# Seven PSUM banks of an attention loop as two slots for maxima and three single-head banks

## What is computed

```python
tokens = x.reshape(B, C, N).transpose(0, 2, 1)
qkv = (tokens @ w_proj + b_proj).reshape(B, N, NUM_HEADS, 3 * HEAD_DIM)
q, k, v = jnp.split(qkv, 3, axis=-1)
attn = jnp.einsum('bihd,bjhd->bijh', q, k) * SCALE
attn = jax.nn.softmax(attn, axis=2)
res = jnp.einsum('bijh,bjhd->bihd', attn, v).reshape(B, N, NUM_HEADS * HEAD_DIM)
out = res @ w_out + b_out + tokens
```

## Time and profile before

| | us |
|---|---|
| median of 3 runs | 3099.82 (3094.11 to 3104.37) |
| the profiled execution | 3101.73 |
| its span | 3100.0 |
| TensorE busy | 2708.6 |
| VectorE busy | 2196.4 |
| ScalarE busy | 1220.1 |
| GpSimd busy | 603.8 |
| mean granted TensorE clock | 0.935 of full |

### The profile page before, as it was taken

The page is one execution under the profiler, slowest core; times in us unless marked ns, Lnnn a source line. Parts: engine busy times, 40 slices in busy tenths (PEclk is TensorE's granted clock), DMA queues, the critical chain, the costliest instruction groups (busy, mean ns, idle before and its releaser), DMA issues.

```text
span 3100.0 us, 42243 instructions
## 1 busy us (share of the span) xinstructions
PE 2708.6 (87%) x14966; PEld 1854.5 (60%) x14966; DVE 2196.4 (71%) x2490; ACT 1220.1 (39%) x1348; POOL 603.8 (19%) x381
## 2 busy tenths in 40 slices
PE   5989979899898898988889888898888899888993
PEld 4447754577545775467754677447764477644772
DVE  4876678766687676867678576785678766787666
ACT  2443325433254333543335333353334533245334
POOL 0520116002160022500224002330024200242011
PEclk8999989999799998999989999899999999899996
DMA  6100050000500005000040001400022000310016
GB/s 154 27 25 1 1 130 1 25 1 14 117 1 25 1 14 117 1 25 1 21 110 1 25 1 38 93 7 19 1 69 62 25 1 1 94 37 25 1 55 244
DMA packets 46388, 124.57 MB, mean 40 GB/s; under 512 B 9792, under 2 KB 21312, under 8 KB 42560
## 3 DMA queue, kind: packets, MB, share of 16 engines
q1 hardware_dynamic: 46144, 121.41, 14.4%
HBM read 43.01 MB, written 23.86 MB: 22 GB/s over the span
## 4 chain that ended last, share of the span: by engine, by line
PE 69%; DVE 10%; ACT 8%; issue 6%; SPq 4%; DMA 3%; DVEq 0%; ACTq 0%
PE tile L1270 23%; PE pv L1270 10%; PE pv L1374 7%; PE tile L1364 6%; PE tile L1342 5%; ACT p L666 4%; PE tile L1515 4%; SPq L452 3%; PE tile L1394 3%; DMA stack<-qk_r 2%; DVE small L877 2%; PE tile L1537 2%; PE tile L1645 2%; PE tile L1564 1%; PE tile L1416 1%
## 5 line engine op out<-in xcount | busy, mean ns | idle before, releaser
L877 DVE TENSOR_REDUCE small<-tile 128x1 f32<-128x1024 f32 x512 | 612.6, 1220 | 125.0 <-PE tile L1342 121.1
L666 ACT ACTIVATE p<-tile 128x1024 f32<-128x1024 f32 x512 | 506.7, 1026 | 457.9 <-PE tile L1364 393.4
L1342 PE MATMUL tile<-stack 96*128 96x512 f32 x1024 | 356.9, 441 | 63.6 <-DMA stack<-qk_r 30.3
L1364 PE MATMUL tile<-stack 112*128 112x512 f32 x1024 | 369.0, 452 | 20.8 <-DVE small L877 14.1
L1270 PE MATMUL tile<-qk_r 128*128 128x512 f32 x1536 | 377.9, 395 | 0.0
L578 POOL TENSOR_TENSOR row_sum<-act 128x256 f32<-128x256 f32 x32 | 42.1, 1335 | 1640.0 <-DVE act L1105 1640.0
L553 POOL TENSOR_TENSOR acc<-acc,p 128x1024 f32<-128x1024 f32 x144 | 344.8, 2416 | 31.2 <-DVE acc L909 29.3
L1270 PEld LDWEIGHTS tile<-qk_r 128*128 128x128 f32 x1536 | 287.1, 188 | 66.4 <-issue 7.7
L1110 DVE TENSOR_TENSOR pl<-p,ph 128x1024 fp32r<-128x1024 f32 x128 | 158.2, 1236 | 238.0 <-ACT p L751 238.0
L1364 PEld LDWEIGHTS tile<-stack 112*128 112x128 f32 x1024 | 175.2, 196 | 241.7 <-issue 85.0
L1342 PEld LDWEIGHTS tile<-stack 96*128 96x128 f32 x1024 | 185.9, 202 | 187.2 <-ACT p L666 110.8
(11 more groups left out here) (277 smaller groups left out, 4256.0 us busy)
## 6 DMA issues: line engine op xcount, KB each, us to landing
stack<-qk_r SPq DMA_DIRECT2D x192, 256.0 KB, 5.0
x_in<-in_x_dram SPq DMA_DIRECT2D x9, 1024.0 KB, 7.6
act<-in_x_dram SPq DMA_DIRECT2D x8, 1024.0 KB, 8.0
x_scratch<-act SPq DMA_DIRECT2D x7, 1024.0 KB, 4.0
z_scratch<-zbuf SPq DMA_DIRECT2D x7, 1024.0 KB, 5.1
stack<-ones SPq DMA_DIRECT2D x8, 512.0 KB, 7.6
w3f<-w3f_scratch SPq DMA_DIRECT2D x8, 512.0 KB, 3.2
fin_rest<-z_scratch SPq DMA_DIRECT2D x3, 1024.0 KB, 12.7
```

Of the source, the lines that this page charges most:

```text
L666: sc.activation(p0[:, jt % DEPTH, pair, :], tile_wait(b, "st0", *u, jt, pair), ACT.Exp, scale=float(D) ** -0.5).then_inc(scalar_done, scal ...
L877: ve.tensor_reduce(maxima[:, h * NT + it:h * NT + it + 1], t[:], X, ALU.max).then_inc(vector_done, vector.one("max0", g, h, it))
L1342: ins = mm(o[:, s], stack[0:IMAX, 0, g, h, it * P:(it + 1) * P], stack[0:IMAX, 1, g, h, s], start=True, stop=True)
L1364: ins = mm(o[:, halves[k]], stack[0:K0, 1, g, h, jt * P:(jt + 1) * P], stack[0:K0, 0, g, h, halves[half]], start=True, stop=True)
```

## The change

- The loop's scores of the first three units are tiles of one head, 128x512, one bank. They rotate over three banks: the two of `tile[2]` and the half of `pv` that the unit doesn't write. `exp0` follows, four a key tile. The last unit keeps pairs.
- Maxima tiles `s0`, and with them the loop's `m0`, `den0` and `ex0`, alternate between `tile[0]` and `tile[1]`. Everything outside the loop, with the last unit, rotates over three tiles as before.
- The order in a key tile is score, score, maximum, maximum, score, score, values.
- `max_rows` on VectorE keeps heads 0 and 1; ScalarE writes heads 2 and 3 in four `max_cols` of 16x256, each with a column of `mask8` as its scale. The maxima's tile is free when both are through.
- `pv0_out` and `max_cols` precede the unit's exponentials on ScalarE.
- `res_lo` moves from VectorE to GpSimd, behind its adds of tile 1, except for the last unit's. Its wait for `res_hi` moves with it.
- The bias of the values is left out of `res_hi` and `res_lo`; its product with the output weights is made once in the setup (4 matmuls, one add, `bvo0`) and added in `x1`.

```diff
+def score_tiles(g, half):
+
+    return 2 if (g, half) == UNITS[-1] else G
...
+def key_tile(g, half):
+
+    if next_unit(g, half):
+        return ("st0", 0), ("st0", 1), ("s0", 0), ("s0", 1), ("st0", 2), ("st0", 3)
+    return ("st0", 0), ("st0", 1)
...
     for u in UNITS:
+        s += [("pv0_out", *last_unit(*u))] if last_unit(*u) else []
+        s += [("max_cols", *u, t) for t in range(HT)]
         for jt in range(NT):
-            s += [("pv0_out", *last_unit(*u))] if last_unit(*u) and jt == 0 else []
-            s += [("exp0", *u, jt, pair) for pair in range(2)]
+            s += [("exp0", *u, jt, k) for k in range(score_tiles(*u))]
             s += [("res_hi", *last_unit(*u))] if last_unit(*u) and jt == 2 else []
...
-            s += [("res_lo", *last)] if last and jt == 3 else []
         if following:
             s += [(n, *following) for n in ("neg_hi", "neg_copy", "neg_lo")]
-            s += [("max_rows", *following, h) for h in range(G)]
+            s += [("max_rows", *following, h) for h in range(G // 2)]
...
 def pool_steps():
-    s = [("add0", *u, jt, pair) for u in UNITS for jt in range(NT) for pair in range(2)
-         if adder(*u, jt, pair) == "pool"]
+    s = []
+    for u in UNITS:
+        for jt in range(1, SUMMED):
+            s += [("add0", *u, jt, pair) for pair in range(2) if adder(*u, jt, pair) == "pool"]
+            s += [("res_lo", *last_unit(*u))] if last_unit(*u) and jt == 1 else []
...
+    home, rings = {}, {"whole": 0, "rows": 0, "scores": 0}
+    for n in tiles:
+        kind, unit, looped = n[0], n[1:3], False
+        if kind in ("st0", "den0"):
+            looped = unit != UNITS[-1]
+        elif kind == "s0":
+            looped = n[3] // HT + n[1] > 0
+        elif kind == "m0":
+            looped = unit != UNITS[0]
+        elif kind == "ex0":
+            looped = next_unit(*unit) not in (None, UNITS[-1])
+        ring = ("scores" if kind == "st0" else "rows") if looped else "whole"
+        if ring == "scores":
+            home[n] = ((2, 0), (2, 1), (3, 1 - n[2]))[rings[ring] % 3]
+        else:
+            home[n] = (rings[ring] % (2 if ring == "rows" else SLOTS), None)
+        rings[ring] += 1
...
+                        if jt == 1 and last_unit(*u):
+                            g, half = last_unit(*u)
+                            cols_ = slice(half * HALF, (half + 1) * HALF)
+                            pool.wait_ge(scalar_done, scalar.at(b, "res_hi", g, half))
+                            pe.tensor_tensor(side[:, 1, g, cols_], raw[:, cols_], side[:, 0, g, cols_].bitcast(F32),
+                                             ALU.subtract).then_inc(pool_done, gps.one("res_lo", g, half))
...
+                def max_cols(g, half):
+
+                    m = tile_wait(b, "m0", g, half)[0:NMAX, HALF:HALF + G // 2 * P].rearrange("p (h n) -> p h n", n=P)
+                    for t in range(HT):
+                        it = HT * half + t
+                        sc.activation(stack[IMAX:K0, 0, g, G // 2:G, it * P:(it + 1) * P], m, ID, scale=mask8[:, it:it + 1]
+                                      ).then_inc(scalar_done, scalar.one("max_cols", g, half, t))
...
-                def st0(g, half, jt, pair):
-
-                    if g == 0 and half == 0 and jt == 0 and pair == 0:
+                def st0(g, half, jt, k):
+
+                    if g == 0 and half == 0 and jt == 0 and k == 0:
                         pe.wait_ge(key_ones_in, 16 * b + 16)
-                    o = free("st0", g, half, jt, pair)
-                    for k in range(2):
-                        h = 2 * pair + k
-                        if jt == 0:
+                    if home["st0", g, half, jt, k][0] == SLOTS and jt == 0 and last_unit(g, half):
+                        scalar_wait("pv0_out", *last_unit(g, half))
+                    o = free("st0", g, half, jt, k)
+                    for q, h in enumerate(heads_of(g, half, k)):
+                        if jt == 0 and h < G // 2:
                             vector_wait("max_rows", g, half, h)
-                        ins = mm(o[:, halves[k]], stack[0:K0, 1, g, h, jt * P:(jt + 1) * P],
+                        elif jt == 0 and h == G // 2:
+                            scalar_wait("max_cols", g, half, HT - 1)
+                        ins = mm(o[:, halves[q]], stack[0:K0, 1, g, h, jt * P:(jt + 1) * P],
                                  stack[0:K0, 0, g, h, halves[half]], start=True, stop=True)
```

More of the change, by code:

```diff
@@ L244, in conv_seq_kernel, with banks, leavers @@
     place = {n: k for k, n in enumerate(tiles)}
-    def slot(*name):
-        return place[name] % SLOTS
-    def leaver(b, *name):
-        k = place[name]
-        former = tiles[k - SLOTS] if k >= SLOTS else [n for n in tiles if slot(*n) == k][-1]
-        engine, *step = last_reader(former)
-        steps = {"scalar": scalar, "vector": vector}[engine]
-        return engine, (steps.at if k >= SLOTS else steps.before)(b, *step)
+    home, rings = {}, {"whole": 0, "rows": 0, "scores": 0}
[15 more added lines that the diff above has]
+        rings[ring] += 1
+    def slot(*name):
+        assert home[name][1] is None
+        return home[name][0]
+    def banks(name):
+        k, half = home[name]
+        return [(k, q) for q in range(2) if half in (None, q)]
+    def leavers(b, *name):
+        k, found = place[name], {}
+        for bank in banks(name):
+            users = [n for n in tiles[k + 1:] + tiles[:k] if bank in banks(n)]
+            if bank[0] == SLOTS:
+                users = [n for n in tiles[:k] if bank in banks(n) and n[1:3] == name[1:3]]
+            for engine, *step in last_readers(users[-1]) if users else ():
+                steps = {"scalar": scalar, "vector": vector}[engine]
+                now = place[users[-1]] < k
+                found[engine] = max(found.get(engine, (False, 0, None)), (now, steps.place[tuple(step)], tuple(step)))
+        return [(engine, ({"scalar": scalar, "vector": vector}[engine].at if now
+                          else {"scalar": scalar, "vector": vector}[engine].before)(b, *step))
+                for engine, (now, _, step) in found.items()]
     x_v = x.rearrange("b (t p) h w -> b p t (h w)", p=P)
@@ L595, in tile_wait @@
                 act_e.wait_ge(tensor_done, tensor.at(b, *name))
-                return tile[slot(*name)][:]
+                return where(*name)
             act_e.wait_ge(weights_in[0], 16)
@@ L686, in _ @@
                     last = last_unit(*u)
+                    if last:
+                        pv0_out(*last)
+                    max_cols(*u)
                     for jt in range(NT):
-                        if last and jt == 0:
-                            pv0_out(*last)
-                        for pair in range(2):
-                            exp0(u, jt, pair)
+                        for k in range(score_tiles(*u)):
+                            exp0(u, jt, k)
                         if last and jt == 2:
@@ L939, in res_lo @@
                     s = slice(half * HALF, (half + 1) * HALF)
-                    STT(side[:, 1, g, s], raw[:, s], col("bv0", g), f(side[:, 0, g, s]), ALU.add, ALU.subtract
-                        ).then_inc(vector_done, vector.one("res_lo", g, half))
+                    TT(side[:, 1, g, s], raw[:, s], f(side[:, 0, g, s]), ALU.subtract
+                       ).then_inc(vector_done, vector.one("res_lo", g, half))
                 def x1(k):
@@ L991, in _ @@
                                 add0(u, jt - 1, pair)
-                        if last and jt == 3:
-                            res_lo(*last)
                     if following:
@@ L1321, in free @@
                 def free(*name):
-                    engine, count = leaver(b, *name)
-                    pe.wait_ge(scalar_done if engine == "scalar" else vector_done, count)
-                    return tile[slot(*name)]
+                    for engine, count in leavers(b, *name):
+                        pe.wait_ge(scalar_done if engine == "scalar" else vector_done, count)
+                    return where(*name)
                 kts = range(CT)
```

85 lines of the change are left out of this document (55 added, 30 removed).

## The result

| | median of | us | range |
|---|---|---|---|
| before, same chip | 4 runs | 3102.1 | 3094.11 to 3104.51 |
| after | 4 runs | 3166.06 | 3160.3 to 3169.06 |

The ratio is 1.0209, 95% interval 1.0184 to 1.0233: slower by 2.1%. The forecast was 3178, range 3098 to 3205. The profiled execution of after has a span of 3167.3 us, 67.3 over that of before.

A forecast was written before the change was run, and what follows sets the result against it. The prediction took TensorE and GpSimd to be in balance. Its terms, 7.0 us a batch, gave 56 for eight, 57 with setup; 3101.7 + 57 + 20 for the clock = 3178 us, range 3098 to 3205.

The forecast's parts named there:

- The score pipeline gets faster, and GpSimd's chain ends the unit all the same: First layer's middle units: key tiles 3.03 us, scores 2.9 earlier, but GpSimd ends 2.2 later; each unit loses 2.0.
- The moved low half: GpSimd, middle units: operation of 1.28 us after standing 1.75 for ScalarE's high half; GpSimd ends at 27.5.
- VectorE's add can't run beside GpSimd's: Unit ends: VectorE's last add waits for GpSimd's eighth, starts at 27.5; next unit at 35.1 us.
- the second rival: First layer's units: both engines' adds run beside each other and scores decide, -3.05 us a batch, 3078; chance 0.12.
- The first rival: Three unit ends: VectorE gets in before GpSimd's eighth add, 57 us come back, 3102, no change; chance 0.13.
- The first unit, +1.95: Start of a batch: ScalarE's four maxima writes delay GpSimd's chain of adds, +1.95 us.
- 24 unit ends: Before the transposes, three units in each of eight batches: new TensorE hole of 2.7 us, clock cost 0 to 40.
- The last unit, +1.2: Last unit's first score takes the denominator's slot and waits for the reciprocal, +1.2 us (0 to 1.2).
- The clock, 20 us: Half-rate TensorE stretches behind the new holes: 0 to 40 us, half of them taken, 20.
- the sum without the clock: All units of a batch: 1.95 + 2.0 + 2.0 + 1.2 - 0.2 = 7.0 us, 56 for eight, 57 with setup.

The follow-up runs named there:

- nine adds: Changed kernel with nine of a unit's adds on GpSimd, VectorE's only one behind the maxima, low half behind all adds, early maxima writes, whole-bank ring rotated: 3039.64 us.
- the turned ring: Changed kernel with VectorE's last add behind the maxima, low half behind all adds, early maxima writes, whole-bank ring shifted by one at the last unit: 3092.85 us.
- the kernel before repaired: Kernel before, banks and order kept: nine GpSimd adds, VectorE's only one behind the negation, low half on GpSimd behind it, bias folded away: 3119.53 us.
- the negation unblocked: Against the run with all ten adds on GpSimd: GpSimd's low half also waits until VectorE's negation of the maxima has ended; 3066.47 us.
- the late add: Changed kernel with VectorE's last add moved behind the last maxima and their negation in the three units with a successor; 3124.48 us.

## Why the prediction was right, by its steps

**The score pipeline gets faster, and GpSimd's chain ends the unit all the same.** Right. Key tiles of the middle unit start 3.06 apart (3.03 predicted), tile 6 at 19.46 (19.4 predicted), and the unit was longer. Putting the low half back gave the middle units 2.65 each; nine adds on GpSimd with the late one behind gave 4.4 and 5.7, of which 1.2 are the turned ring's.

**The moved low half**: 1.28 and a stand of 1.75 were predicted, 1.29 and 1.82 measured; GpSimd's end 27.5 predicted, 27.1 measured. Most of the 0.4 is the middle add: I had GpSimd stand 1.15 for it; instead its six adds run on and take 14.99, 0.83 more than six of 2.36. For unit (0, 1) 35.1 was predicted (27.5 + 4.22 + 3.29 is 35.0) and 35.07 measured, and that is luck. Where the lower clock cost nothing the unit is 34.4 long, 1.3 over before and not 2.0: GpSimd ends earlier, and from its end to the transposes it is 3.98 and not 4.22, since the blocked add is over 1.09 after GpSimd. The other five batches are longer by their clock, which the sum had in another term.

**VectorE's add can't run beside GpSimd's.** Right: 3.20 beside one, 1.22 alone. That also settles the second rival (both run, 3078). The first rival (VectorE gets in before the eighth add, 3102) did not happen by itself; made to happen by a wait it gave 3123, since the middle add still holds the maxima. The Trainium skill (SBUF — State Buffer, Who interferes with whom) counts tensor_scalar among the VectorE instructions that can contend with GpSimd, in a mode that takes both of VectorE's ports; the negation of 1.60 and 2.84 agrees, though no run shows its mode.

**The first unit, +1.95.** The cause was right, and GpSimd's last add ends 1.95 later as predicted (29.73 against 27.79 in the mean). The transposes follow 1.6 later; the other 1.15 of the +2.75 are clock: in six of eight batches the lower level stands behind the hole of 2.3 before them. The prediction counted that hole among its 24 unit ends. Taking the cause away gave 3.8, more than the term, since TensorE had stood for the four writes as well.

**The last unit, +1.2.** Right: 1.22, shown by the turned ring.

**The clock, 20 us.** The size came out, the place only in part. Compared with like units of the same trace that lack the low stretch: at 11 of the 24 unit ends the lower level stands behind the hole, and from the transposes to the next first score it takes 4.7 to 5.0 instead of 3.29 (6.1 to 6.2 instead of 4.51 where the reciprocal's wait is in it), 17 us in all. In five more middle units the low stretch inside the unit is twice as long, and they are 0.65 longer (35.0 against 34.4, 36.25 against 35.6), 3 us. That is an estimate by difference, and chance has a part in how near it is, since I had put all holes at unit ends. In all 16 middle units TensorE stood inside the unit as well, for the maxima behind VectorE's middle add (1.26 and 0.40), in 11 of them the half-clock stretch then lay there, and in six of these it cost nothing to be seen, since TensorE had slack before the end (a hole of 0.7 was still left).

**What made 3178 too high** is the sum without the clock. Without those 20 us the units are 5.1 a batch over before, where 7.2 was predicted: the middle ones 34.4 and 35.6 instead of 35.1 and 36.4, the first +1.6 instead of +1.95, the last -0.24 instead of 0 (not explained). That is 17 us too much for eight batches. Some 7 us went the other way: the first score of all (+1.8, not +1), the rest of a batch (+0.13, not -0.2) and the last batch's end (3).

## What to carry to other kernels

An engine with 19% busy time can set the length of a loop: look in the timeline of one iteration at who ends last, and count each instruction that is moved onto that engine with the stand that it makes. Before a VectorE instruction with two SBUF operands, or a small tensor_scalar, goes next to GpSimd's work, ask what is queued behind it; here it paid to give GpSimd more adds so that VectorE has none in the middle, and to put the one left behind the maxima. When scores get faster, rebalance the helpers in the same step: the banks with one operation moved to the wrong engine cost 2.1%, without that move still 1.2%, with the adds reordered they gained 1.9%.

## What the runs showed of the hardware that I had not expected

- A tensor_scalar of 128x16 (0.17 us alone) waited 2.67 us for GpSimd, through one add and the instruction queued behind it, and 1.43 when that one was held back. It did not get in between the two, as VectorE's middle add does, which waited 2.18 (3.40 less 1.22), under one add, with further adds queued. What makes the difference stays open.
- Holes of 1.5 to 1.8 us before the transposes were never followed by the lower level, 1.2 GHz, in the denominator; those of 2.75 to 2.86 always were. Those of 2.3 to 2.4 went either way: in the changed kernel 11 of 12 were followed by it, in the run with the low half back 4 of 7. The twelfth, in the first unit of the seventh batch of the changed kernel:

```profile
2426.79 0.60 PE L1440 MATMUL tile<-ident,small 128*16 128x128 f32 x4 [2.36 <-DVE small L972]
2427.32 1.08 PE L1486 MATMUL tile<-acc,segment 128*32 128x128 f32 x32
```

  So the price of a hole is not a function of its length alone; 1.25 us less of hole was worth 2.9 where it crossed from one case to the other.
- The same work behind the first layer took 253.6 to 256.8 us a batch, as means of one kernel and another, 0.94 and 0.93 of clock in the two windows shown. With the turned ring this hid some 9 us, with the kernel before repaired it added 12.
- The step from one batch's first score to the next takes few values: 368.2 to 369.0 with nine adds, 371.9 to 372.3 with the negation unblocked (but for one), 375.1 to 375.7 in most batches of the kernel before and all with the turned ring, 378.3 to 379.3 in most batches of six other runs, however much their units differ. With the late add the second batch's units sum to 124.06 and the step is 379.0; with the kernel before repaired they sum to 122.49 and the step is 378.7. So totals here tend to move in steps of some 27 us, and a gain in one stage is read from that stage. Why the steps gather was not tried.
